# Rows of maxima turned by a transposing DMA, and the last maxima combined right behind the last unit

## The chip, the cores and the metric

The kernel runs on one core of a Trainium2 chip. The metric is the device time of one execution in microseconds; the kernel before took 875.57 us (median of 3 runs, 874.52 to 877.58). Engines: TensorE (PE; PEld its weight loads), VectorE (DVE), ScalarE (ACT), GpSimd (POOL) and SyncE (SP), which here issues every DMA.

## The reference, cut to what matters

```python
x = L0_attn_x                       # (4, 1024, 256) f32
xn = layernorm(x)
q, kv = rotary(heads(xn @ Wq)) * 16 ** -0.5, rotary(heads(xn @ Wkv))    # 16 heads of 16
att = einsum('bmd,bnd->bmn', q, kv)             # 1024 x 1024 for each of 64 (batch, head)
out = softmax(att) @ kv                          # keys are the values too
ffn = (silu(xn @ wg.T) * (xn @ wu.T)) @ wd.T     # hidden 768, dequantised int weights
return x + out @ Wout + bout + ffn
```

## The kernel before

The front part (to about 230 us) runs over 8 chunks of 512 tokens: layernorm, projections, rotary tables and the whole feed-forward. The projected q and k are split into two 16-bit parts each and stored to DRAM. The rest is the attention, and it is this part that the change is about.

**Pairs and steps.** The 64 (batch, head) items go by in 32 pairs (`PAIRS`), two heads at a time on different rows of TensorE. A pair has 8 steps (`STEPS`), one for each tile of 128 keys, and each step two halves of 512 queries. So a pair has 16 half steps. A half step on TensorE (`step`, L777) is: `scores` (L703, matmuls L716), a part of `values` (L734, probabilities times values) and `maxima` (L740, matmuls L751).

**Why maxima.** The softmax subtracts each query's maximum before the exponential. The maxima are made by a first pass over the scores with the queries on the partitions: `maxima` on TensorE, then one VectorE reduce of 128 x 1024 per unit (L1137), 16 units a pair. This pass runs 12 steps (`LEAD`) ahead of the second. So unit 15 of pair p + 1 stands in half step 7 of pair p (counted from 0), and behind it start the units of pair p + 2. VectorE's `combine` (L1142, the operation L1147) folds the two halves of the keys into `rowmax`. In the kernel before, `combine` of a pair stands behind the first reduce of the following pair.

**How the maxima reach the scores.** GpSimd's `split_max` (L1291) writes `rowmax` as three 16-bit parts into 48 columns of `mparts` (six small operations, L1299 to L1309). The parts must become rows of `qs`, where they are multiplied by unit rows in `ks`, so that the score matmul of 51 rows gives score minus maximum. The turn is done by `turn_max` (L649) on TensorE with an identity, in step 6 (`T_AT`) of the pair before, behind the values of half step 12. It goes into a score bank. ScalarE's `rows` (L915, operation L922) copies 48 rows out to `mrows`, and SyncE's `load_mrows` (L372, two DMAs at L377) puts them into `qs` and raises `m_in`. `scores` waits for `m_in` once a pair, before its first half step.

**Banks.** Scores rotate over three PSUM banks, 4 to 6 (`score_bank`, L344). `place` (L333) numbers everything that takes one: two places for each half step, one for the turn (`turn_place`, L338) and, from pair 10 (`LAG`) on, one for an output tile (`tile_place`, L341). `free` (L686) makes TensorE wait until the use three places ago is read: an exponential, a copy of the turned rows or a copy of a tile. The banks 0 to 3 are for maxima, bank 7 for the values.

**ScalarE** does 32 exponentials a pair (L972), a copy of the pair's outputs (L986) in step 1, and from pair 10 on the copy of a tile (L992). **VectorE** does also one small reciprocal a pair (`invert`, L1192, operation L1197) in step 4.

**SyncE** works through one fixed list (`slot`, L465), in this order for pair p: loads of an output tile's parts (`load_tile`, L400, from pair 10 on); `load_pair` of pair p + 2; `store_o` of pair p - 1; `store_inv` of pair p - 1 (waits for the reciprocal); `store_res` of a tile; `load_mrows` of pair p + 1. GpSimd multiplies the tile's parts (L1339); TensorE projects the tile in half step 3 (L759).

Of the kernel before, what the change touches and what calls it, by code (L numbers as in the profile page):

```python
# [23 lines left out]
FP16 = mybir.dt.float16  # L24
# [30 lines left out]
M_UNIT = (2.0 ** 15, 2.0 ** 5, 1.0)  # L55
MAXES = 2 * BT
LEAD = 12
T_AT = 6
INV_AT = 4
COPY_O_AT = 1  # L60
TILE_SLOT = 3
# [7 lines left out]
QH = SEQ // CHUNK  # L69
PER_STEP = 2 * QH  # L70
PBUF = 4
TURN_INDEX = PER_STEP * T_AT + 2
TILE_INDEX = 2 * (TILE_SLOT + 1)
WHOLE = None
VALUES = {PBUF + n: divmod(n, 2) for n in range(2 * STEPS)}
# [11 lines left out]
def build(nc, x, w_q, w_kv, w_out, b_out, w_gate, w_up, w_down, rope, ident, out):  # L87
# [10 lines left out]
    with ExitStack() as ctx:  # L98
# [78 lines left out]
        munit = sb("munit", [P, 4, 2, BT], F32)  # L177
        mrest = sb("mrest", [P, 2, BT], F32)
        mparts = [sb(f"mparts{i}", [P, P], FP16) for i in range(2)]
        mrows = [sb(f"mrows{i}", [MPARTS * MAXES, P], FP16) for i in range(2)]  # L180
        used[0] = 0
        probs = [carve(CHUNK, F32) for _ in range(PBUF * PER_STEP)]
        vstage = [carve(2 * BT * 2 * DH, F32, "p (a k n) -> p a k n", a=2, k=BT) for _ in range(2)]
# [74 lines left out]
        msplit = sem("msplit")  # L258
        msplit_done = sem("msplit_done")
        mturned = sem("mturned")  # L260
        mrows_done = sem("mrows_done")
        m_in = [sem(f"m_in{i}") for i in range(RING)]
        scores_done = sem("scores_done")
        exp_done = sem("exp_done")
# [63 lines left out]

        def pair_base(p):

            return (PER_STEP * STEPS + 1) * p + max(p - LAG, 0)

        def place(p, kt, j):  # L333

            n = PER_STEP * kt + j
            return pair_base(p) + n + (n >= TILE_INDEX) * with_tile(p) + (n >= TURN_INDEX) * (p + 1 < PAIRS)

        def turn_place(p):  # L338
            return pair_base(p) + TURN_INDEX + with_tile(p)

        def tile_place(p):  # L341
            return pair_base(p) + TILE_INDEX
# [5 lines left out]
        def _(sp):  # L348
# [10 lines left out]
            def load_pair(p, ring):  # L359
# [4 lines left out]
                for a in range(2):  # L364
# [3 lines left out]
                    for tile, first, part in ((qs, 0, q[0:DH, :]), (qs, DH, q), (ks, 0, k), (ks, 2 * DH, k[0:DH, :])):  # L368
                        n = part.shape[0]
                        sp.dma_start(tile[ring][top + first:top + first + n, :], part).then_inc(stacks_in[ring], 16)  # L370

            def load_mrows(p, slot):  # L372
                sp.wait_ge(mrows_done, p + 1)
                n = MPARTS * BT
                for a in range(2):
                    top = HEAD_ROWS * a + PROD
                    sp.dma_start(qs[slot % RING][top:top + MPARTS, :], mrows[slot % 2][a * n:(a + 1) * n, :]  # L377
                                 ).then_inc(m_in[slot % RING], 16)

            def store_o(p, slot):  # L380
# [68 lines left out]
                load_pair(p, p)  # L449
            for c in range(CPB, NCHUNK):  # L450
                if c + 1 == NCHUNK:
                    load_mrows(0, 0)
                store_chunk(c // CPB, c % CPB)

# [10 lines left out]
            def slot(p, j, load, rows, tiles):  # L465

                for b, t, n, k in tiles:
                    sp.wait_ge(divided, CREDIT + n - 1)
                    if n is tiles[0][2]:

                        m = (j + 1) % 2
                        sp.wait_ge(inv_stored[m], 16 * QH * ((p - 3 - m) // 2 + 1))
                    load_tile(b, t, k)
                if p == PAIRS - 2:
                    sp.wait_ge(inv_stored[0], 16 * QH * (PAIRS - RING) // 2)
                    load_last(0, front_in)
                if load:
                    if not isinstance(p, int) or p >= 2:
                        sp.wait_ge(scores_done, QH * STEPS * (p - 1))
                    load_pair(p + 2, (j + 2) % RING)  # L480
                if not isinstance(p, int) or p >= 1:
                    store_o(p - 1, j - 1)
                if not isinstance(p, int) or p >= 1:
                    store_inv(p - 1, j - 1)
                for b, t, n, k in tiles:
                    store_res(b, t, n, k)
                if rows:
                    load_mrows(p + 1, j + 1)
# [40 lines left out]
        def _(pe):  # L529
# [60 lines left out]
            def turn_qk(c):  # L590

                pe.wait_ge(rope_done, CT * (c + 1))
                if c < NCHUNK - 1:
                    pe.wait_ge(xl_ready, KD * (c + 2))
                else:
                    pe.wait_ge(mrows_done, 1)
                for g in range(4):
                    if g == 2:
                        pe.wait_ge(silu_done, KH * c + 5)
                        pe.wait_ge(hid_done, KH * c + 5)  # L600
                    for t in range(CT):
                        mm = pe.transpose(bank_turn(g)[:, t * P:(t + 1) * P], qk[:, t, g * P:(g + 1) * P], identf[:, :])  # L602
                    mm.then_inc(turned, 1)
# [42 lines left out]
                                   ks[pl][top:top + PROD, h * CHUNK:(h + 1) * CHUNK], start=True, stop=True)  # L646
                mm.then_inc(max_scores, 1)

            def turn_max(p, slot_of, before, bank):  # L649

                pe.wait_ge(msplit_done, p + 1)
                pe.wait_ge(*before)
                pe.transpose(ps[:, bank, 0:P // 2].bitcast(FP16), mparts[slot_of % 2][:, :], identh[:, :]
                             ).then_inc(mturned, 1)

            pe.wait_ge(ident_in, 16)
            turn_x(0)
            pe.wait_ge(wqkv_in, 32)
# [3 lines left out]
            for c in range(NCHUNK):  # L662
                project(c)
                if c == 0:
                    pe.wait_ge(wsum_done, 2)
                else:
                    for t in range(CT):
                        down(c - 1, t)
                gate_up(c, 0)
                gate_up(c, 1)  # L670
                if c + 1 < NCHUNK:
                    turn_x(c + 1)
                else:
                    pe.wait_ge(identh_ready, 1)
                    turn_max(0, 0, (y_done, CT * c), 4)
                units = lead_units(c)
                for j in range(2, KH):
                    if units:
                        if j == 2:
                            pe.wait_ge(rope_read, CT * (c + 1))  # L680
                        lead(units[j - 2])
                    gate_up(c, j)
                turn_qk(c)


            def free(p, first, last):  # L686

                exps = 0
                for n in range(max(first, 0), last + 1):
                    q = p - (n < pair_base(p))  # L690
                    if q + 1 < PAIRS and n == turn_place(q):
                        pe.wait_ge(mrows_done, q + 2)
                    elif with_tile(q) and n == tile_place(q):
                        pe.wait_ge(wout_copied, q - LAG + 1)
                    else:
                        k = n - pair_base(q)
                        k -= with_tile(q) and k > TILE_INDEX
                        k -= q + 1 < PAIRS and k > TURN_INDEX
                        exps = PER_STEP * STEPS * q + k + 1
                if exps:  # L700
                    pe.wait_ge(exp_done, exps)
# [75 lines left out]
            def step(turn, ls, last_turn=False):  # L777
# [5 lines left out]
                for half in range(2):  # L783
# [6 lines left out]
                        values(of, pair, *block)  # L790
                    elif p == 0 and slot:
                        if slot == 1:
                            pe.wait_ge(y_done, CT * NCHUNK)
                        for k in range(KD):
                            pe.matmul(ps[:, 7, :], identh[:, :], wg[:, k, 0:CHUNK], start=True, stop=True)
                    if p + 1 == PAIRS:
# [6 lines left out]
                            project_tile(n, n % 2, 0)  # L803
                        if slot in FRONT_AT:
                            project_front(FRONT_AT[slot])
                    if slot == 2 * T_AT and p + 1 < PAIRS:
                        turn_max(p + 1, pl + 1, (exp_done, PER_STEP * (STEPS * p + T_AT)), score_bank(turn_place(p)))
                    if slot == TILE_SLOT and with_tile(p):
                        free(p, tile_place(p) - 3, tile_place(p) - 3)
                        project_tile(p - LAG, (p - LAG) % 2, score_bank(tile_place(p)))  # L810
# [51 lines left out]
        def _(act):  # L862
# [52 lines left out]
            def rows(p, slot, turn, bank):  # L915

                act.wait_ge(mturned, p + 1)
                if not (isinstance(p, int) and p < 2):

                    act.wait_ge(m_in[(slot - 2) % RING], 32 * (turn + (slot - 2) // RING + 1))  # L920
                n = MPARTS * MAXES
                act.activation(mrows[slot % 2][:, :], ps[0:n, bank, 0:P // 2].bitcast(FP16), ACT.Copy  # L922
                               ).then_inc(mrows_done, 1)

            roots(0, CT)
            normalise(0)
            roots(CT, 2 * CT)
# [4 lines left out]
            for c in range(NCHUNK):  # L932
# [7 lines left out]
                high(c, 0)  # L940
                if more:
                    copy_x(c + 1, 0)
                else:
                    rows(0, 0, 0, 4)
                high(c, 1)
                silu(c, 2)
                if more:
# [13 lines left out]
            def exps(turn, ls):  # L961
# [5 lines left out]
                for j in range(PER_STEP):  # L967
# [10 lines left out]
                    if j == 1 and kt == T_AT and p + 1 < PAIRS:  # L978
                        rows(p + 1, pl + 1, turn, score_bank(turn_place(p)))

            def copy_o(p, slot, turn):

# [22 lines left out]
        def _(dve):  # L1005
# [125 lines left out]
            def maxima(turn, m, h, bank):  # L1131
# [4 lines left out]
                dve.wait_ge(max_scores, n + 1)  # L1136
                dve.tensor_reduce(negmax[pl % 2][:, h, :, kt], ps[:, bank:bank + 2, :],  # L1137
                                  AX.X, ALU.max, negate=True).then_inc(max_done, 1)
                if k == 0 and not (isinstance(p, int) and p == 0):
                    combine(p - 1, pl - 1)  # L1140

            def combine(p, pl):  # L1142

# [59 lines left out]
            def step(turn, ls, last_turn=False):  # L1203
                m = ls + LEAD
                q = ls // STEPS
                if not last_turn or m < RING * STEPS:
                    maxima(turn, m, 0, 0)
                    maxima(turn, m, 1, 2)
                if last_turn and m == RING * STEPS:
                    combine(PAIRS - 1, RING - 1)  # L1210
# [42 lines left out]
        def _(pool):  # L1253
# [37 lines left out]
            def split_max(p, slot):  # L1291

                pool.wait_ge(rowmax_done, p + 1)
                if not (isinstance(p, int) and p < 2):
                    pool.wait_ge(mturned, p - 1)
                rm = rowmax[slot % 2][:, :, :]
                mp = mparts[slot % 2][:, 0:2 * MPARTS * BT].rearrange("p (a k i) -> p a k i", a=2, k=MPARTS)
                n = 5 * p
# [119 lines left out]
```

## Time and profile before

| | |
|---|---|
| time, median of 3 | 875.57 us |
| profiled execution | 875.66 us |
| its span | 873.9 us |
| granted TensorE clock, mean | 0.996 |
| busy: PE, DVE, ACT, POOL | 836.4, 762.1, 692.8, 187.2 us |
| chain that ended last: PE, ACT, DVE | 66%, 24%, 4% of the span |
| VectorE reduces L1137 | 512, 1217 ns mean, 596.2 us |
| ScalarE exponentials L972 | 1024, 595 ns mean, 557.8 us |
| TensorE values L734, scores L716, maxima L751 | 326.5, 198.2, 190.2 us |
| SyncE waited for the copy of the turned rows, before L377 | 46.3 us in 32 times |
| SyncE waited for the reciprocal, before L397 | 182.8 us in 30 times |

An operation's busy time is that of the engine; its mean may be longer than the time from one start to the next, since an instruction begins before the one ahead of it has ended. The loop's half steps are regular, so the distance of equal rows (start to start) tells the cost better than the durations.

### The profile page before, as it was taken

To read this page: it belongs to the slowest core of one execution; us is meant where nothing else is said; L and a number is where in the kernel's file an instruction comes from. 1 tells how busy PE (TensorE), PEld (TensorE's weight loads), DVE (VectorE), ACT (ScalarE), POOL (GpSimd) and SP (SyncE) were. 2 spreads that over 40 slices of the span, in tenths; PEclk is the share of its full clock that TensorE was granted. 3 is DMA by queue.
4 is the path that set the end of the run, shared out by engine and by line. 5 is a ranking of instruction groups with operands and counts; after the bars stand their busy time and mean duration, and the time that the engine had idled before them with its cause. 6 is when DMAs were issued, how large, how long until landed. Compare 5 with 4: busy or idle time off the path is not lost.

```text
span 873.9 us, 19473 instructions
## 1 busy us (share of the span) xinstructions
PE 836.4 (96%) x7488; PEld 326.0 (37%) x7488; DVE 762.1 (87%) x936; ACT 692.8 (79%) x1303; POOL 187.2 (21%) x411
## 2 busy tenths in 40 slices
PE   4898999999999999999999999999999999999998
PEld 2465555555433333333333333333333333333334
DVE  6897888788799999999999999999999999999902
ACT  4545445433799999999999999999999999999983
POOL 4523344435210000001111111111111111111210
PEclk9899999999999999999999999999999999999999
DMA  9112110011201111111112211111111221111222
GB/s 316 47 50 78 57 50 27 23 49 49 67 26 28 35 37 27 32 28 27 45 49 55 57 50 50 46 46 45 45 51 51 53 57 49 50 46 46 75 75 79
DMA packets 58498, 47.46 MB, mean 54 GB/s; under 512 B 18189, under 2 KB 48717, under 8 KB 58405
## 3 DMA queue, kind: packets, MB, share of 16 engines
q1 hardware_dynamic: 58404, 46.20, 18.1%
q8 instruction: 60, 0.98, 0.5%
q14 instruction: 34, 0.27, 0.1%
HBM read 28.57 MB, written 16.90 MB: 52 GB/s over the span
## 4 chain that ended last, share of the span: by engine, by line
PE 66%; ACT 24%; DVE 4%; issue 4%; POOL 0%; ACTq 0%; DVEq 0%
ACT arena L972 23%; PE ps L734 20%; PE ps L751 11%; PE ps L716 11%; PE ps L585 7%; PE ps L613 4%; PE ps L759 3%; PE ps L562 2%; PE ps L564 1%; PE ps L563 1%; PE ps L602 1%; PE ps L645 1%; DVE stats L1013 1%; DVE negmax L1137 1%; DVE side L1071 1%
## 5 line engine op out<-in xcount | busy, mean ns | idle before, releaser
L1137 DVE TENSOR_REDUCE negmax<-ps 128x2 f32<-128x1024 f32 x512 | 596.2, 1217 | 31.8 <-PE ps L751 27.7
L972 ACT ACTIVATE arena<-ps 128x512 f32<-128x512 f32 x1024 | 557.8, 595 | 49.4 <-PE ps L716 25.8
L734 PE MATMUL ps<-arena 128*32 128x256 f32 x4072 | 326.5, 392 | 2.2 <-issue 2.0
L716 PE MATMUL ps<-qs,ks 51*128 51x512 f16 x1024 | 198.2, 382 | 9.6 <-ACT arena L972 8.6
L751 PE MATMUL ps<-ks,qs 48*128 48x512 f16 x976 | 190.2, 386 | 0.0
L734 PEld LDWEIGHTS ps<-arena 128*32 128x32 f32 x4072 | 80.3, 107 | 122.6 <-issue 121.5
L751 PEld LDWEIGHTS ps<-ks,qs 48*128 48x128 f16 x976 | 46.7, 92 | 188.5 <-issue 183.2
L899 ACT ACTIVATE side<-ps 128x512 f32<-128x512 f32 x48 | 28.7, 597 | 94.8 <-PE ps L585 94.8
L585 PE MATMUL ps<-arena,side 128*128 128x512 f16 x384 | 89.0, 380 | 0.2
L716 PEld LDWEIGHTS ps<-qs,ks 51*128 51x128 f16 x1024 | 51.6, 93 | 91.5 <-ACT arena L972 53.8
L1299 POOL TENSOR_TENSOR mparts<-rowmax,munit 128x16 f16<-128x16 f32 x32 | 7.6, 238 | 291.8 <-DVE rowmax L1147 291.8
L1277 POOL TENSOR_TENSOR side<-side 128x512 f16<-128x512 f32 x48 | 55.9, 1167 | 61.1 <-ACT side L905 60.3
L585 PEld LDWEIGHTS ps<-arena,side 128*128 128x128 f16 x384 | 35.4, 98 | 44.4 <-issue 6.3
L1339 POOL TENSOR_TENSOR arena<-arena 128x256 f32<-128x256 f32 x24 | 17.5, 730 | 158.2 <-DMA arena<-inv_d 158.2
L1071 DVE SCALAR_TENSOR_TENSOR side<-ps,side 128x512 f32<-128x512 f32 x48 | 32.9, 690 | 16.0 <-PE ps L585 9.5
L905 ACT ACTIVATE side<-side 128x512 f16<-128x512 f32 x48 | 30.0, 625 | 13.5 <-DVE side L1071 13.3
L613 PE MATMUL ps<-side 128*128 128x256 f16 x336 | 37.8, 273 | 0.0
L613 PEld LDWEIGHTS ps<-side 128*128 128x128 f16 x336 | 32.9, 98 | 5.3
L1344 POOL TENSOR_TENSOR arena<-arena,x_all 128x256 f32<-128x256 f32 x22 | 16.1, 731 | 64.6 <-ACT arena L992 64.6
L759 PE MATMUL ps<-wo,arena 128*128 128x256 f32 x96 | 27.1, 405 | 0.0
L562 PE MATMUL ps<-arena 128*128 128x512 f16 x56 | 22.2, 397 | 4.5 <-DVE side L1071 4.5
L1077 DVE TENSOR_TENSOR arena<-ps,arena 128x512 f16<-128x512 f32 x32 | 19.8, 682 | 7.1 <-ACT arena L913 7.1
(101 smaller groups left out, 522.7 us busy)
## 6 DMA issues: line engine op xcount, KB each, us to landing
parts_d<-arena SPq DMA_DIRECT2D x64, 128.0 KB
x_all<-x_dram SPq DMA_DIRECT2D x8, 512.0 KB, 8.8
qs<-parts_d SPq DMA_DIRECT2D x64, 64.0 KB, 1.9
ks<-parts_d SPq DMA_DIRECT2D x64, 64.0 KB, 1.9
o_d<-arena SPq DMA_DIRECT2D x124, 32.0 KB
arena<-o_d SPq DMA_DIRECT2D x24, 128.0 KB
arena<-inv_d SPq DMA_DIRECT2D x48, 64.0 KB
out_dram<-arena SPq DMA_DIRECT2D x24, 128.0 KB, 1.8
```

The lines of the kernel that those rows point to most:

```text
L562: pe.matmul(bank_proj(t), hi, wqkv_hi[:, k, :], start=(k == 0), stop=False)
L585: mm = pe.matmul(bank, w[:, k, j * P:(j + 1) * P], xp[:, k, :], start=(n == 0), stop=(n == 2 * KD - 1))
L613: mm = pe.matmul(bank_down(c, t), hp[:, n % KH, t * P:(t + 1) * P], wd[:, n % KH, :], start=(n == 0), stop=(n == 2 * KH - 1))
L716: mm = pe.matmul(ps[:, score_bank(place(p, kt, 2 * half + a)), :], ks[ring][top:top + ROWS, kt * P:(kt + 1) * P], qs[ring][top:top + ROWS, ...
L734: mm = pe.matmul(ps[32 * j:32 * j + 32, 7, cols], vstage[pl % 2][:, j % 2, kt, :], probs[PER_STEP * (kt % PBUF) + j][:, cols], start=(kt = ...
L751: mm = pe.matmul(ps[:, 2 * h + a, :], qs[ring][top:top + PROD, kt * P:(kt + 1) * P], ks[ring][top:top + PROD, h * CHUNK:(h + 1) * CHUNK], ...
L759: mm = pe.matmul(ps[:, bank, 0:DIM], atile[k][:, g, :], wo[:, g, :], start=(g == 0), stop=(g == HG - 1))
L905: act.activation(hh[:, j, :], hid[j % 3][:, :], ACT.Copy).then_inc(hh_done, 1)
L972: act.activation(probs[PER_STEP * (kt % PBUF) + j], ps[:, score_bank(place(p, kt, j)), :], ACT.Exp).then_inc(exp_done, 1)
L1071: dve.scalar_tensor_tensor(hid[j % 3][:, :], bank_up(j), DEQUANT * H_SCALE, gact[j % 2][:, :], ALU.mult, ALU.mult).then_inc(hid_done, 1)
L1137: dve.tensor_reduce(negmax[pl % 2][:, h, :, kt], ps[:, bank:bank + 2, :], AX.X, ALU.max, negate=True).then_inc(max_done, 1)
L1277: pool.tensor_tensor(hl[:, j, :], hid[j % 3][:, :], hh[:, j, :], ALU.subtract).then_inc(hl_done, 1)
```

## The change

The turn on TensorE and ScalarE's copy go, and with them their place in the rotation of banks. In their stead SyncE issues one transposing DMA of the whole 128 x 128 16-bit tile `mparts` into `mrows` (`turn_rows`), from SBUF to SBUF. It waits for `split_max` and, from pair 2 on, for the load that read this `mrows` before. It stands in SyncE's list behind `store_o` and ahead of `store_inv`. `load_mrows` now waits for the DMA's landing (`mturned`, 16 a time). GpSimd's guard before it writes `mparts` again waits for the same semaphore. VectorE's `combine` now stands right behind unit 15 of its own pair; it waits for that very reduce. In the front part the last chunk loses a turn and a copy, and `turn_rows(0, 0)` goes ahead of `load_mrows(0, 0)`.

```diff
-T_AT = 6
-TURN_INDEX = PER_STEP * T_AT + 2
@@
-        mrows = [sb(f"mrows{i}", [MPARTS * MAXES, P], FP16) for i in range(2)]
+        mrows = [sb(f"mrows{i}", [P, 1, P], FP16) for i in range(2)]
@@
         def pair_base(p):
-            return (PER_STEP * STEPS + 1) * p + max(p - LAG, 0)
+            return PER_STEP * STEPS * p + max(p - LAG, 0)
         def place(p, kt, j):
             n = PER_STEP * kt + j
-            return pair_base(p) + n + (n >= TILE_INDEX) * with_tile(p) + (n >= TURN_INDEX) * (p + 1 < PAIRS)
+            return pair_base(p) + n + (n >= TILE_INDEX) * with_tile(p)
@@ SyncE
+            def turn_rows(p, slot):
+                sp.wait_ge(msplit_done, p + 1)
+                if p >= 2:
+                    sp.wait_ge(m_in[(slot - 2) % RING], 32 * ((p - 2) // RING + 1))
+                sp.dma_start_transpose(mrows[slot % 2][:, :, :], mparts[slot % 2][:, :]).then_inc(mturned, 16)
             def load_mrows(p, slot):
-                sp.wait_ge(mrows_done, p + 1)
+                sp.wait_ge(mturned, 16 * (p + 1))
@@
                 if not isinstance(p, int) or p >= 1:
                     store_o(p - 1, j - 1)
+                if rows:
+                    turn_rows(p + 1, j + 1)
                 if not isinstance(p, int) or p >= 1:
                     store_inv(p - 1, j - 1)
@@ TensorE: turn_max and its two calls go; turn_qk of the last chunk
-                    pe.wait_ge(mrows_done, 1)
+                    pe.wait_ge(y_done, CT * c)
@@ TensorE, free
-                    if q + 1 < PAIRS and n == turn_place(q):
-                        pe.wait_ge(mrows_done, q + 2)
@@ ScalarE: rows and its two calls go
@@ VectorE, maxima
-                if k == 0 and not (isinstance(p, int) and p == 0):
-                    combine(p - 1, pl - 1)
+                if k + 1 == MAXES:
+                    combine(p, pl)
@@ GpSimd, split_max
-                    pool.wait_ge(mturned, p - 1)
+                    pool.wait_ge(mturned, 16 * (p - 1))
```

## Rows read from the trace of the kernel before

**Rows 1.** The page, busy us (share of the span) and instructions of each engine

```profile
PE 836.4 (96%) x7488; PEld 326.0 (37%) x7488; DVE 762.1 (87%) x936; ACT 692.8 (79%) x1303; POOL 187.2 (21%) x411
```

**Rows 2.** Windows: stretch, length, busy us by engine, granted clock, DMA share, GB/s

```profile
300.00:400.00 100.00, 97.75 (x1014) 30.26 (x1014) 98.02 (x95) 94.22 (x180) 9.56 (x43) 1.00 0.12 30
500.00:600.00 100.00, 98.78 (x997) 32.47 (x995) 94.10 (x91) 92.95 (x178) 16.29 (x50) 1.00 0.19 50
```

**Rows 3.** Timeline of ScalarE: start, us, engine, line, operation, tiles, count

```profile
320.64 0.26 ACT L922 ACTIVATE mrows<-ps 48x128 f16<-48x128 f16 x1
339.68 0.26 ACT L922 ACTIVATE mrows<-ps 48x128 f16<-48x128 f16 x1
...
494.97 0.26 ACT L922 ACTIVATE mrows<-ps 48x128 f16<-48x128 f16 x1
...
514.75 0.26 ACT L922 ACTIVATE mrows<-ps 48x128 f16<-48x128 f16 x1
```

**Rows 4.** Timeline of TensorE around the turn of a tile pair

```profile
507.68 0.39 PE L716 MATMUL ps<-qs,ks 51*128 51x512 f16 x2
...
513.30 0.38 PE L716 MATMUL ps<-qs,ks 51*128 51x512 f16 x2
...
514.18 0.23 PE L653 MATMUL ps<-identh,mparts 128*128 128x128 f16 x1
...
514.92 0.39 PE L716 MATMUL ps<-qs,ks 51*128 51x512 f16 x2 [0.19 <-ACT arena L972]
...
518.41 0.39 PE L716 MATMUL ps<-qs,ks 51*128 51x512 f16 x2
```

**Rows 5.** Timeline of VectorE, in the same pair and at the start

```profile
507.89 2.35 DVE L1137 TENSOR_REDUCE negmax<-ps 128x2 f32<-128x1024 f32 x2
...
511.28 0.17 DVE L1147 TENSOR_TENSOR rowmax<-negmax 128x16 f32<-128x16 f32 x1
511.36 1.22 DVE L1137 TENSOR_REDUCE negmax<-ps 128x2 f32<-128x1024 f32 x1
512.50 0.24 DVE L1197 RECIPROCAL arena<-arena 128x16 f32<-128x16 f32 x1
512.65 3.42 DVE L1137 TENSOR_REDUCE negmax<-ps 128x2 f32<-128x1024 f32 x3
...
7.03 0.18 DVE L1022 RECIPROCAL rstd<-std 128x4 f32<-128x4 f32 x1 [0.36 <-ACT std L865]
7.24 0.16 DVE L1024 SCALAR_TENSOR_TENSOR shift<-mv,rstd 128x4 f32<-128x4 f32 x1
```

**Rows 6.** Timeline of TensorE in a pair without a tile

```profile
328.81 0.38 PE L716 MATMUL ps<-qs,ks 51*128 51x512 f16 x2
...
330.35 0.39 PE L716 MATMUL ps<-qs,ks 51*128 51x512 f16 x2
```

**Rows 7.** Timeline of GpSimd

```profile
511.52 0.22 POOL L1299 TENSOR_TENSOR mparts<-rowmax,munit 128x16 f16<-128x16 f32 x1 [6.26 <-DVE rowmax L1147]
...
513.02 0.22 POOL L1309 TENSOR_TENSOR mparts<-mrest,mwhole 128x16 f16<-128x16 f32 x1
...
520.96 0.73 POOL L1339 TENSOR_TENSOR arena<-arena 128x256 f32<-128x256 f32 x1 [7.25 <-DMA arena<-inv_d]
```

**Rows 8.** Timeline of SyncE's queue: the time is that of issuing

```profile
512.76 1.15 SPq L397 DMA_DIRECT2D inv_d<-arena  x2
513.96 0.43 SPq L415 DMA_DIRECT2D out_dram<-arena  x1
515.04 1.54 SPq L377 DMA_DIRECT2D qs<-mrows  x2
...
517.12 1.33 SPq L407 DMA_DIRECT2D arena<-inv_d  x2
```

**Rows 9.** DMA issues by line, whole execution: count, KB each, median us to landing

```profile
qs<-parts_d SPq DMA_DIRECT2D x64, 32.0 KB, 1.8
```

**Rows 10.** Timeline, weight loads of the next tile's projection

```profile
522.69 0.73 PEld L759 LDWEIGHTS ps<-wo,arena 128*128 128x128 f32 x4 [0.41 <-ACT arena L972]
```

More of the change, by code:

```diff
@@ L260, in build @@
         mturned = sem("mturned")
-        mrows_done = sem("mrows_done")
         m_in = [sem(f"m_in{i}") for i in range(RING)]
@@ L329, in pair_base @@
         def pair_base(p):
-            return (PER_STEP * STEPS + 1) * p + max(p - LAG, 0)
+            return PER_STEP * STEPS * p + max(p - LAG, 0)
         def place(p, kt, j):
             n = PER_STEP * kt + j
-            return pair_base(p) + n + (n >= TILE_INDEX) * with_tile(p) + (n >= TURN_INDEX) * (p + 1 < PAIRS)
-        def turn_place(p):
-            return pair_base(p) + TURN_INDEX + with_tile(p)
+            return pair_base(p) + n + (n >= TILE_INDEX) * with_tile(p)
         def tile_place(p):
@@ L376, in load_mrows @@
                     top = HEAD_ROWS * a + PROD
-                    sp.dma_start(qs[slot % RING][top:top + MPARTS, :], mrows[slot % 2][a * n:(a + 1) * n, :]
+                    sp.dma_start(qs[slot % RING][top:top + MPARTS, :], mrows[slot % 2][a * n:(a + 1) * n, 0, :]
                                  ).then_inc(m_in[slot % RING], 16)
@@ L451, in _ @@
                 if c + 1 == NCHUNK:
+                    turn_rows(0, 0)
                     load_mrows(0, 0)
@@ L647, in lead @@
                 mm.then_inc(max_scores, 1)
[L649 to L654, printed above, removed]
             pe.wait_ge(ident_in, 16)
@@ L672, in _ @@
                     turn_x(c + 1)
-                else:
-                    pe.wait_ge(identh_ready, 1)
-                    turn_max(0, 0, (y_done, CT * c), 4)
                 units = lead_units(c)
@@ L690, in free @@
                     q = p - (n < pair_base(p))
-                    if q + 1 < PAIRS and n == turn_place(q):
-                        pe.wait_ge(mrows_done, q + 2)
-                    elif with_tile(q) and n == tile_place(q):
+                    if with_tile(q) and n == tile_place(q):
                         pe.wait_ge(wout_copied, q - LAG + 1)
@@ L697, in free @@
                         k -= with_tile(q) and k > TILE_INDEX
-                        k -= q + 1 < PAIRS and k > TURN_INDEX
                         exps = PER_STEP * STEPS * q + k + 1
@@ L792, in step @@
                         if slot == 1:
+                            pe.wait_ge(identh_ready, 1)
                             pe.wait_ge(y_done, CT * NCHUNK)
@@ L805, in step @@
                             project_front(FRONT_AT[slot])
-                    if slot == 2 * T_AT and p + 1 < PAIRS:
-                        turn_max(p + 1, pl + 1, (exp_done, PER_STEP * (STEPS * p + T_AT)), score_bank(turn_place(p)))
                     if slot == TILE_SLOT and with_tile(p):
@@ L913, in high_qk @@
                     act.activation(parts[g][:, 0, :], bank_turn(g), ACT.Copy).then_inc(hi_done, 1)
[L915 to L923, printed above, removed]
             roots(0, CT)
@@ L942, in _ @@
                     copy_x(c + 1, 0)
-                else:
-                    rows(0, 0, 0, 4)
                 high(c, 1)
@@ L977, in exps @@
                         copy_tile(p - LAG, (p - LAG) % 2, score_bank(tile_place(p)))
-                    if j == 1 and kt == T_AT and p + 1 < PAIRS:
-                        rows(p + 1, pl + 1, turn, score_bank(turn_place(p)))
             def copy_o(p, slot, turn):
@@ L1208, in step @@
                     maxima(turn, m, 1, 2)
-                if last_turn and m == RING * STEPS:
-                    combine(PAIRS - 1, RING - 1)
                 if ls % STEPS == INV_AT and (q or not isinstance(turn, int)) and not (last_turn and q == RING - 1):
```

## The prediction

> **What bounds the kernel now.** I read the page first. PE is busy in nearly the whole span, DVE and ACT follow [rows 1]. That share doesn't name the bound, so I read windows next. In 300 to 400 us (head pairs 0 to 9, which have no output tile) PE is busy 97.75 and DVE 98.02 of 100 us: two engines near the limit. In 500 to 600 us (with tiles) PE has 98.78, DVE only 94.10 [rows 2]. The granted clock is 1.00, the 2.4 GHz level, in both, so the clock is no term of the sum.
>
> Then the period. ScalarE's copy of the turned maxima comes once a pair: every 339.68 - 320.64 = 19.04 us without a tile and every 514.75 - 494.97 = 19.78 us with one [rows 3]. A pair is 16 half steps: scores, values, maxima. TensorE's timeline shows what a half step costs and what the turn adds. From 507.68 to 513.30 five half steps take 5.62 us, 1.124 each. The four that follow, the turn in the first, take 518.41 - 513.30 = 5.11 us in place of 4.50: 0.61 us extra, though the transpose itself is 0.23 us long [rows 4]. The rest is a wait: the turn takes one of the three score banks, so the scores at 514.92 stood for ScalarE ("<-ACT arena L972"). They needed an exponential that is one later than usual.
>
> **The change, part by part.**
>
> 1. *The turn and its copy go (31 times in the loop, pairs 0 to 30; each serves the next pair).* The gain on TensorE lies between 0.50 us (the turn's own half step, 514.92 - 513.30 = 1.62 against 1.12) and 0.61 us (all four) [rows 4]. Slower half steps stand only behind the turn, so I take 0.57. ScalarE also loses its 0.26 us copy [rows 3]; it is not the bound, so this counts nothing beyond the bank that comes free sooner.
>
> 2. *What is late next, tile pairs.* VectorE: back to back, two reduces take 2.35 us and one takes 1.22, so each costs 1.13; the combine costs 511.36 - 511.28 = 0.08 and the reciprocal 512.65 - 512.50 = 0.15 [rows 5]. That is 16 x 1.13 + 0.23 = 18.31 us a pair, under 19.78 - 0.57 = 19.21. TensorE stays the bound and the 0.57 is kept: 21 pairs x 0.57 = 12.0 us.
>
> 3. *Pairs without a tile.* TensorE needs 16 x 1.124 plus what the copy of the outputs makes it wait once (330.35 - 328.81 = 1.54 against 1.12, 0.42) [rows 6]: 18.40 us. VectorE needs 18.31 plus the new wait of item 4, 18.43. The two are level, and each holds up the other now and then; I take 18.52, a gain of 0.52 of 19.04. Ten pairs: 5.2 us.
>
> 4. *The combine right behind the last unit.* It now waits for the reduce issued just ahead of it; before, the next pair's first reduce stood between. Queued behind the wait is that reduce, and TensorE's maxima two units on wait for it. The nearest row of such a self-wait is the reciprocal at 7.03, 0.18 long, with its reader at 7.24: 0.03 us after its end, where neighbours without a wait overlap by 0.09 (512.74 against 512.65) [rows 5]. So 0.12 us a pair on VectorE, bounds 0 and 0.15; hidden in tile pairs by the slack of item 2, counted in item 3. In return the row maxima are there one reduce earlier.
>
> 5. *The transposing DMA, which no row shows.* I follow the chain in the tile pair at 510 us. The last reduce of the next pair ends at 507.89 + 2.35 = 510.24 [rows 5]. Combine, 0.03 + 0.17: 510.44. GpSimd's split starts 0.07 later (511.52 after 511.28 + 0.17) and takes 513.02 + 0.22 - 511.52 = 1.72 [rows 7]: 512.23. SyncE issues at 512.27. The load of the turned rows has two issues, 1.54 us together [rows 8]; the second starts 0.77 in and lands as a small load does, 1.8 to 1.9 us on [rows 9]: 2.7 us. The next pair's scores, at 518.41 before, are wanted at 518.41 - 0.60 = 517.81; less 2.7 and 0.1 for the semaphore, the load must start by 515.0. So the transposition may take 2.7 us from issue to landing. Everything beyond stalls TensorE one for one in all 31 pairs, as it waits in order and nothing can take the slot. Lower bound of its latency: 1.8 us, the load of a similar size [rows 9]. Upper bound: the slowest landing inside the loop, the broadcast load, issued from 517.12 and used at 520.96 by GpSimd, 3.8 us [rows 7, 8]. The size is 32 KB, nearest to the 32 KB load, and it has no HBM side; the reordering costs something. I take 2.4 us: no stall.
>
> What I set beside this: the DMA load of 32 KB lands in 1.8 us [rows 9]. The Trainium skill ("VectorE: DVE Perf Modes", The three transpose paths) gives 1309 ns for a 128 x 128 16-bit transpose by DMA and 390 ns on TensorE, and advises TensorE where PSUM will do, so it speaks against the change; "DMA: Bandwidth & Descriptors", Anatomy of one DMA, gives about 2.0 us of fixed cost, for another issuing path than SyncE's; no run here shows either figure yet. Added, an estimate from these pages is 3.3 us, a stall of 0.6 us a pair, and the sum would come to about 877.
>
> 6. *SyncE's queue.* The transposition stands ahead of store_inv, store_res and load_mrows. It is issued at 512.27, before the 512.76 at which store_inv began [rows 8], and takes between 0.43 us (the issue of store_res, at 513.96) and 0.77 (half of the load's 1.54). So store_inv moves to 513.0 at the latest, store_res ends by 514.7, and the load still finds the queue free by 515.0. The next tile's loads follow the load of the rows as before; its product is ready at 520.96 + 0.73 = 521.69, and TensorE wants it at 522.69 [rows 7, 10]. Of the 1.0 us of slack the shorter pair takes 0.6. Nothing for the queue, then; its cover is gone if the issue takes over 1.1 us, after which it is a stall like item 5's. GpSimd's new wait (the transposition of two pairs before) is two periods, some 38 us, old: free.
>
> 7. *The first part.* One transposition and one copy go from the last chunk: at most 0.23 + 0.26 us, I take 0.3. The new load is issued earlier there, long before pair 0 starts.
>
> **The sum.** The profiled execution took 875.66 us (span 873.9 and 1.8 around it), 0.1 over the median of 875.57. 875.66 - 12.0 - 5.2 - 0.3 = 858.2 us.
>
> **The rivals.**
>
> *A transposition somewhat slow.* At 3.0 us the stall is 0.3 us in 31 pairs: 9.3 us back, 867.5. It gives between all and almost none of the gain back as the latency goes from 2.7 to 3.3. For it: the move rearranges 16-bit elements; against it: plain small transfers land at 1.8 to 1.9, so 0.8 us more is needed before anything shows. The Trainium skill's figures, added as above, fall at its upper end.
>
> *A transposition so slow that the kernel loses.* The gain of 17.5 us is used up by a stall of 0.56 us, a latency of 3.3; from 3.4 on the kernel is measurably slower than before. At the 3.8 us of the slowest landing it stalls 1.1 us x 31 = 34 us: 892. Its place is the first scores of each pair, the wait for m_in. For it: the budget of 2.7 is a chain without any slack, which was 0.6 us with the copy through PSUM; the transposition and the load are two landings in series where one was. Against: it needs twice a small load's latency.
>
> *VectorE becomes the bound everywhere.* If the self-wait costs far more than 0.15 us, the pairs without tile gain only half, 2.6 us less: 861. It stays inside the forecast's range.
>
> *The change does little* because the 0.61 us is not the turn's: then half steps 13 to 16 stay at 1.15 and the gain is 0.50 a pair, 31 x 0.50 + 0.3 = 15.8: 859.9; also within it.
>
> **How the numbers follow.** No stall (the last two included): 0.50, with 856.5 to 863 as its own range (0.60 in all 31 pairs gives 875.66 - 18.6 - 0.5 = 856.6). Somewhat slow: 0.25. Slow enough to lose: 0.25. About 0.3%, 2.6 us, is what a measurement of this kernel can tell from no change. Faster by more holds all of the first and 0.20 of the second: 0.70. Within 0.3%: 0.05 of the second and 0.01 of the third, 0.06. Slower: 0.24. The range runs from 856.5 to 886; its upper end is a stall of 0.9 us (858.2 + 27.9), a latency of 3.6, and beyond it I leave 0.17, with 0.02 below.
>
> **What would show it.** In the profile after, the copies of the output banks should lie 18.5 us apart early and 19.2 us later, all 16 half steps at 1.12, no wait of the scores for "DMA qs<-mrows", the split about 1.0 us earlier in the pair, and VectorE near 98% in both parts. A wait of L716 for that DMA, once a pair, is the stall; its length plus 2.7 is the transposition's latency. If SyncE's row for the new issue is longer than 1.1 us, item 6 is wrong. If the gap at 514 us is gone but the slots behind stay at 1.15, item 1's upper part is.

## The result

The changed kernel takes 870.16 us (median of 7 runs, 867.68 to 872.65), the kernel before took 877.58 us in the same comparison (7 runs). The ratio is 0.993 with a 95% interval of 0.9914 to 0.9946: faster by 0.7%, 5 to 8 us; the two medians lie 7.4 us apart. Forecast were 858.2 us and a gain of 17.5. So the sign and the range held, and more than half of the gain is missing. The question is where it went.

The page of the changed kernel's profile (its execution took 867.68 us), busy time by engine and the chain that ended last:

```profile
span 865.9 us, 19347 instructions
...
PE 826.8 (95%) x7456; PEld 320.8 (37%) x7456; DVE 758.0 (88%) x936; ACT 688.0 (79%) x1271; POOL 185.9 (21%) x411
...
PE 71%; DVE 15%; DMA 3%; SPq 2%; issue 2%; ACT 2%; POOL 2%; DVEq 0%; ACTq 0%; POOLq 0%
```

Against [rows 1], PE is busy 9.6 us less. New in the chain is DMA with SyncE's queue, 5% of the span: something that TensorE waits for is now a transfer. ScalarE's 24% of before is down to 2%. TensorE's score matmuls wait for an exponential 9 times where they did 40 times before, 31 fewer: the wait behind the turn, once a pair, is gone. Windows of the same two stretches as in [rows 2]:

```profile
300.00:400.00 100.00, 97.67 (x1028) 29.94 (x1028) 98.51 (x98) 94.79 (x177) 9.12 (x41) 1.00 0.14 32
500.00:600.00 100.00, 98.97 (x998) 32.46 (x998) 94.36 (x92) 93.39 (x176) 16.88 (x51) 1.00 0.20 52
```

More matmuls fit into the head pairs' 100 us (1028 against 1014), yet both engines show idle time. The list of waits names it (engine, line, waited for: us in total, times, longest):

```profile
PEld ps L743 <- DVE negmax L1114: 109.9, 270, 0.4
...
PEld ps L708 <- DMA qs<-mrows: 14.3, 26, 1.7
...
PE ps L708 <- DMA qs<-mrows: 6.0, 8, 1.3
```

L708 is the score matmul (L716 before), and it waits for the load of the turned rows in nearly every pair. In the kernel before the same wait stood there once, with 0.7 us. The 109.9 us of weight loads that wait for VectorE look worse but cost nothing that shows: they are 0.4 us at most, and the half steps below are no longer for them.

TensorE's timeline at the end of a tile pair, to set beside [rows 4]:

```profile
512.54 0.38 PE L708 MATMUL ps<-qs,ks 51*128 51x512 f16 x2
...
513.68 0.39 PE L708 MATMUL ps<-qs,ks 51*128 51x512 f16 x2
...
514.96 0.39 PE L708 MATMUL ps<-qs,ks 51*128 51x512 f16 x2
...
516.10 0.39 PE L708 MATMUL ps<-qs,ks 51*128 51x512 f16 x2
```

The half steps take 1.14, 1.28, 1.14 us. The one with the turn, 1.62 before, is now 1.14, and the one behind it went from 1.17 to 1.12. The last one before the next pair took 1.17 before the change and takes 1.17 where nothing disturbs it, not the 1.12 that was forecast for all sixteen; here it takes 1.28, and in other pairs up to 2.58. The half steps with other work are as they were: 1.54 with the copy of the outputs, 2.18 and 1.22 with an output tile. Over the 31 pair changes of this execution the surpluses of the last half steps over 1.17 us add up to 9.0 us. Since 867.7 - 9.0 = 858.7, the sum of the forecast is there, and the stalls are what is missing: between the two profiled executions the gain is 8.0 of the 17.5 us, and 9.0 of the 9.5 that are missing are these surpluses. The table sorts them by what the trace shows at the place:

| where | pairs | stall |
|---|---|---|
| pairs 1, 3, 5, 7, 18, 27: the transposition lands 3.3 to 4.0 us after its issue | 6 | 5.1 us |
| pairs 9, 11, 29: its issue takes 1.43 to 1.73 us, in place of 1.14 | 3 | 1.0 us |
| pairs 12 to 17, 20 to 26, 28, 30 (tile pairs): nothing unusual, 0.10 to 0.16 each | 15 | 1.9 us |
| pair 31: GpSimd's split takes 2.5 us | 1 | 1.0 us |
| pairs 2, 4, 6, 8, 10, 19 | 6 | 0 |

For the transposing DMA itself the view of the tile `mrows` gives the issue on SyncE (ns, min/median/max) and the time to landing:

```profile
L371 SPq DMA_TRANSPOSE mrows<-mparts x32: 1119/1143/1728, 204.8 to 822.1; - x32
...
DMA to landing us min/median/max: 2.3/2.3/4.0
```

A median of 2.3 us where I had taken 2.4, but a tail to 4.0; and an issue of 1.14 us where I had taken at most 0.77. What that does to SyncE's queue in a tile pair:

```profile
509.32 1.14 SPq L371 DMA_TRANSPOSE mrows<-mparts  x1
510.51 1.14 SPq L399 DMA_DIRECT2D inv_d<-arena  x2
511.70 0.43 SPq L417 DMA_DIRECT2D out_dram<-arena  x1
512.18 1.55 SPq L379 DMA_DIRECT2D qs<-mrows  x2
```

The rows have landed at 509.32 + 2.3 = 511.6, but SyncE gets to their load only at 512.18, 2.86 us after the issue. The rows are in place 2.73 us later, at 514.91, and the scores start at 514.96. Without a tile there is no L417 row, and the load starts at 2.34.

The combine came out as worked out. VectorE and GpSimd in the same pair:

```profile
503.74 3.49 DVE L1114 TENSOR_REDUCE negmax<-ps 128x2 f32<-128x1024 f32 x3
507.33 0.17 DVE L1124 TENSOR_TENSOR rowmax<-negmax 128x16 f32<-128x16 f32 x1
507.42 2.35 DVE L1114 TENSOR_REDUCE negmax<-ps 128x2 f32<-128x1024 f32 x2
...
509.07 0.22 POOL L1284 TENSOR_TENSOR mparts<-mrest,mwhole 128x16 f16<-128x16 f32 x1
```

The last reduce ends at 507.23; combine and wait take until 507.42. A reduce right behind a reduce would have started 0.09 us before 507.23, so the two cost 0.28 us; the combine alone cost 0.08 before [rows 5]. The self-wait is thus 0.20 us, not 0.12. The split ends at 509.29, 2.06 us after the last reduce (1.99 were forecast), and the issue follows at 509.32.

### The profile page after: what moved, and what is told of

It reads as the page before. It is cut to its first block, busy times and chain, and to the rows that moved or that the text cites. A ratio compares the mean times of both kernels' runs of the same rounds, so it can differ in the third digit from the quotient of the medians.

```text
span 865.9 us, 19347 instructions
## 1 busy us (share of the span) xinstructions
PE 826.8 (95%) x7456; PEld 320.8 (37%) x7456; DVE 758.0 (88%) x936; ACT 688.0 (79%) x1271; POOL 185.9 (21%) x411
## 4 chain that ended last, share of the span: by engine, by line
PE 71%; DVE 15%; DMA 3%; SPq 2%; issue 2%; ACT 2%; POOL 2%; DVEq 0%; ACTq 0%; POOLq 0%
PE ps L726 24%; PE ps L743 13%; DVE negmax L1114 12%; PE ps L708 11%; PE ps L590 8%; PE ps L618 4%; PE ps L751 3%; DMA qs<-mrows 2%; DMA mrows<-mparts 2%; ACT arena L951 2%; PE ps L567 1%; PE ps L568 1%; PE ps L569 1%; PE ps L607 1%; PE ps L650 1%
## 5 line engine op out<-in xcount | busy, mean ns | idle before, releaser
L1114 DVE TENSOR_REDUCE negmax<-ps 128x2 f32<-128x1024 f32 x512 | 589.9, 1212 | 23.8 <-PE ps L743 19.6
L708 PE MATMUL ps<-qs,ks 51*128 51x512 f16 x1024 | 197.8, 382 | 9.6 <-DMA qs<-mrows 6.0
L743 PEld LDWEIGHTS ps<-ks,qs 48*128 48x128 f16 x976 | 46.6, 92 | 198.9 <-DVE negmax L1114 109.9
L708 PEld LDWEIGHTS ps<-qs,ks 51*128 51x128 f16 x1024 | 49.8, 92 | 89.5 <-ACT arena L951 45.1
L567 PE MATMUL ps<-arena 128*128 128x512 f16 x56 | 21.8, 389 | 4.5 <-DVE side L1048 4.5
```

Source lines behind the costliest of these rows:

```text
L567: pe.matmul(bank_proj(t), hi, wqkv_hi[:, k, :], start=(k == 0), stop=False)
L708: mm = pe.matmul(ps[:, score_bank(place(p, kt, 2 * half + a)), :], ks[ring][top:top + ROWS, kt * P:(kt + 1) * P], qs[ring][top:top + ROWS, ...
L743: mm = pe.matmul(ps[:, 2 * h + a, :], qs[ring][top:top + PROD, kt * P:(kt + 1) * P], ks[ring][top:top + PROD, h * CHUNK:(h + 1) * CHUNK], ...
```

## The experiments

**Where the wait comes from: the queue, the chain, or VectorE.** The first moves one entry of SyncE's list.

```diff
@@ slot (SyncE), label e2_load_before_res
-                for b, t, n, k in tiles:
-                    store_res(b, t, n, k)
                 if rows:
                     load_mrows(p + 1, j + 1)
+                for b, t, n, k in tiles:
+                    store_res(b, t, n, k)
```

> The changed kernel with one thing moved: SyncE loads the turned rows ahead of the store of the output tile, not behind it. Theory A (the wait for the rows is what gives the gain back, and in pairs with a tile it is SyncE's queue: the transposition's issue takes 1.14 us, store_inv 1.14 and store_res 0.43, so the load starts 2.86 us after the transposition's issue though that lands after 2.28): the last half step of the 21 tile pairs falls from 1.28 to 1.33 us to 1.17, the load starts 2.34 us after the transposition's issue, and the kernel is 3 to 4 us faster than the changed one, 11 us under the kernel before. The landings of 3.3 to 4.0 us in a few pairs stay, shorter in effect by 0.4. Theory B (the landing of the transposition itself is the bound in every pair): no change, since the queue isn't waited for. Theory C (VectorE, which now waits for its own reduce): no change.

Measured: 866.76 us (6 runs) against 876.48 for the kernel before (17 runs), ratio 0.9885 [0.986, 0.9911]. SyncE's queue in a tile pair, and the waits of the whole kernel:

```profile
490.95 1.14 SPq L371 DMA_TRANSPOSE mrows<-mparts  x1
492.14 1.14 SPq L399 DMA_DIRECT2D inv_d<-arena  x2
493.33 1.55 SPq L379 DMA_DIRECT2D qs<-mrows  x2
494.93 0.42 SPq L417 DMA_DIRECT2D out_dram<-arena  x1
```

```profile
PEld ps L708 <- DMA qs<-mrows: 6.8, 9, 1.6
...
PE ps L708 <- DMA qs<-mrows: 3.9, 5, 1.3
```

The load starts 2.38 us after the issue, and the last half step of an undisturbed tile pair is 1.17. The waits fall from 26 times to 9. Seven last half steps are still long: six behind a late landing and the one before pair 31. The gain over the kernel before is 9.7 us where 11 were expected. Theory A holds for the tile pairs; B and C had expected no change. As ratios to the kernel before, 0.9885 here and 0.993 for the changed kernel, the move is worth 4 us, the upper end of what was expected; the two intervals almost touch, so the trace is the better witness.

**The chain has no slack.** The DMA stays and the combine goes back behind the next pair's first reduce.

```diff
@@ maxima (VectorE), label e3_late_combine
-                if k + 1 == MAXES:
-                    combine(p, pl)
+                if k == 0 and not (isinstance(p, int) and p == 0):
+                    combine(p - 1, pl - 1)
@@ step (VectorE)
+                if last_turn and m == RING * STEPS:
+                    combine(PAIRS - 1, RING - 1)
```

> The changed kernel with the combine back in its old place, behind the next pair's first reduce. Theory A (the chain from the last reduce to the scores has no slack left): the chain starts 0.97 us later and the stall before each pair grows by that, less the 0.5 us of slack in the even pairs without a tile: 31 x 0.97 - 2.5 = 27 us more than the changed kernel, some 20 us over the kernel before. Theory C (the new wait of VectorE is what costs): the kernel gets faster than the changed one by about 0.12 x 31 = 4 us.

Measured: 892.61 us (4 runs), ratio 1.0178 [1.0143, 1.0213]: 16 us slower than the kernel before and 22 slower than the changed one (27 were expected). A pair's first scores and the waits:

```profile
504.71 0.39 PE L708 MATMUL ps<-qs,ks 51*128 51x512 f16 x2 [0.97 <-DMA qs<-mrows]
```

```profile
PEld ps L708 <- DMA qs<-mrows: 37.1, 31, 2.0
...
PE ps L708 <- DMA qs<-mrows: 27.8, 31, 1.7
```

All 31 pairs wait. The last half step is 2.21 to 2.29 us in most tile pairs, 1.05 over the undisturbed 1.17; the stalls add up to 30.8 us, 21.8 more than in the changed kernel. In an undisturbed tile pair that is the one-for-one price of a chain that starts about a microsecond later. The sum stays 5 us under the expectation mostly because pairs 3, 5, 7, 18 and 27 have no late landing of 3 us or more in this run, and because nothing moved in pair 31, which has no pair behind it to wait for. Theory C is out: VectorE's self-wait is gone here, and the kernel is slower.

**The combine alone.** The same move in the kernel before, with the turn on TensorE.

```diff
@@ maxima (VectorE), label e4_combine_only, from the kernel before
-                if k == 0 and not (isinstance(p, int) and p == 0):
-                    combine(p - 1, pl - 1)
+                if k + 1 == MAXES:
+                    combine(p, pl)
@@ step (VectorE)
-                if last_turn and m == RING * STEPS:
-                    combine(PAIRS - 1, RING - 1)
```

> The kernel before with only the combine moved right behind the last reduce of its pair; the turn stays on TensorE. Theory A: nothing, within 1 us of the kernel before, as the turn stands at a fixed place in TensorE's order and the rows had about 0.6 us of slack. Theory C (the self-wait of VectorE costs in each pair): 2 to 4 us slower. The period stays 19.04 and 19.79 us.

Measured: 876.48 us (12 runs), ratio 0.9989 [0.9972, 1.0006]. No change, with periods of 19.04 and 19.79 us. The self-wait does not show, and an earlier combine is worth nothing to a turn that stands at a fixed place of TensorE's order. It is worth 22 us to the DMA. The second half of the change is what makes the first one pay.

**The turn's removal with slack.** The maxima run 13 steps ahead; two more units are done in front, where TensorE and VectorE wait for each other.

```diff
@@ label e6_lead13
-LEAD = 12
+LEAD = 13
@@ TensorE, ahead of down_most of the last chunk
+            pe.wait_ge(silu_done, KH * NCHUNK)
+            pe.wait_ge(hid_done, KH * NCHUNK)
+            maxima(0, LEAD - 1, 0)
+            maxima(0, LEAD - 1, 1)
@@ VectorE, between low_qk and add_ffn of the last chunk
+            maxima(0, LEAD - 1, 0, 0)
+            maxima(0, LEAD - 1, 1, 2)
```

> The changed kernel with the maxima 13 steps ahead in place of 12: the two units more are done before the first step, between the last storing of parts and the last feed-forward sums. So the chain to the rows starts one step, 2.25 us, earlier in each pair. Theory A: no stall before any pair is left, also not where the transposition lands after 3.3 to 4.0 us; the periods are 18.5 and 19.2 us, and the gain of taking the turn from TensorE stands whole: 31 stalls of together 9.0 us go, less 0 to 2.3 us for the two units in front; 16 to 18 us under the kernel before. Theory C: as the changed kernel, 7 us under the kernel before. If TensorE's removed half-step time were only 0.50 us a pair and not 0.60, 13 to 14 us under.

Measured: 859.13 us (5 runs, 857.28 to 861.17), ratio 0.9806 [0.9782, 0.983], 17.3 us under the kernel before. One window of this kernel, the waits of its score matmuls, and SyncE's queue in a tile pair:

```profile
500.00:600.00 100.00, 99.86 (x1022) 32.72 (x1018) 96.19 (x95) 94.86 (x178) 18.08 (x58) 1.00 0.19 51
```

```profile
PEld ps L708 <- ACT arena L955: 46.1, 237, 0.7
...
PEld ps L708 <- issue: 12.2, 58, 0.7
PE ps L708 <- ACT arena L955: 2.1, 9, 0.6
PEld ps L708 <- DVE x_all L1066: 1.0, 1, 1.0
```

```profile
444.94 1.15 SPq L371 DMA_TRANSPOSE mrows<-mparts  x1
447.83 1.15 SPq L399 DMA_DIRECT2D inv_d<-arena  x2
449.02 0.43 SPq L417 DMA_DIRECT2D out_dram<-arena  x1
449.51 1.56 SPq L379 DMA_DIRECT2D qs<-mrows  x2
```

No wait for `mrows` is left, though three transpositions here land after 3.3 to 3.6 us. The reason is in the queue: store_inv waits for its reciprocal until 447.83, 2.89 us after the issue, so a late landing hides behind it. The load lands at 449.51 + 2.73 = 452.24, half a microsecond ahead of the scores at 452.73. The periods are 18.49 and 19.24 us, 0.55 less than before in both kinds of pair, and PE is busy 99.86 of 100. No cost of the two units in front can be seen: pair 0 starts at 229.66 us in this execution and at 229.67 in the kernel before, though between traces with one and the same front part this start moves by up to 2.5 us. This version beats both kernels.

**Is it the earlier maxima that help?** The same 13 steps and early combine with the turn on TensorE and ScalarE.

```diff
@@ label e7_lead13_te: e4_combine_only, and the edit of e6_lead13 (cut to its first lines)
-LEAD = 12
+LEAD = 13
```

> The kernel before (turn on TensorE and ScalarE) with the combine right behind its last reduce and the maxima 13 steps ahead, as in the version with 13 steps and the DMA. If the gain of that version is the turn's removal, this one stays within 2 us of the kernel before, with periods of 19.04 and 19.79 us. If it is the earlier maxima that helped, it is 10 us or more under the kernel before.

Measured: 876.27 us (10 runs) against 876.26, ratio 1.0007 [0.9991, 1.0023]. With the turn on TensorE the 13 steps and the early combine are worth nothing. The 17 us are the turn's removal, once its chain has slack.

**Why some transpositions are late.** The changed kernel again, for a second trace and a comparison on one chip:

> The changed kernel as it is, on the chip of this call. Its time over the kernel before is to be 6 to 8 us less, as before. Theory F (late landings of the transposition come from fetches of instructions): each transposition with a landing above 3.2 us has a 16 KB packet of the instruction queue on a DMA engine that began 0.7 to 1.7 us after the issue, and none of the others has.

Measured: 870.35 us (6 runs), ratio 0.993 [0.9907, 0.9953]. Its stalls add up to 10.1 us. The expectation held only in part. Late landings and fetches of 16 KB go together, but the stated window of 0.7 to 1.7 us was too narrow: pair 1 is late with a fetch at 1.81, pair 25 with one at 2.43, and pair 27, with one at 0.89, lands after 3.01, under the 3.2 that was set. The DMA view of two stretches of the first trace of the changed kernel, each 3.5 us from the issue in pair 3 and pair 4 (queue, kind, packets, MB, share of 16 engines; then the median us to landing):

```profile
q8 instruction: 1, 0.02, 2.2%
...
mrows<-mparts SPq DMA_TRANSPOSE x1, 3.3
```

```profile
q14 instruction: 1, 0.01, 1.0%
...
mrows<-mparts SPq DMA_TRANSPOSE x1, 2.3
```

In pair 3 a fetch of 16 KB of instructions runs as one packet: 2.2% of 16 engines x 3.5 us is 1.2 us on a single DMA engine. By the packet records it began 0.87 us after the transposition's issue and ended at 2.11. The 8 KB fetch in pair 4 did no harm. The packets of the transposition itself show what the fetch does. It moves as 128 packets of 256 bytes and 32 of 4 bytes. The same view of 0.4 us, from 1.1 us after the issue, first in pair 3 and then in pair 4:

```profile
DMA packets 120, 0.03 MB, mean 77 GB/s; under 512 B 120, under 2 KB 120, under 8 KB 120
```

```profile
DMA packets 128, 0.03 MB, mean 82 GB/s; under 512 B 128, under 2 KB 128, under 8 KB 128
```

In pair 3, 8 of the 128 are missing, the share of one DMA engine in 16. They move from 2.10 us on, when the fetch has ended.

The test shifts the fetches: small matmuls ahead of the last feed-forward sums move TensorE's position in its instructions against the work.

```diff
@@ TensorE, ahead of down_most of the last chunk, label e8_pad_te (e9_pad24: 24 in place of 48)
+            pe.wait_ge(identh_ready, 1)
+            pe.wait_ge(silu_done, KH * NCHUNK)
+            pe.wait_ge(hid_done, KH * NCHUNK)
+            for _ in range(48):
+                pe.matmul(ps[:, 1, 0:2], identh[:, :], identh[:, 0:2], start=True, stop=True)
```

> The changed kernel with 48 matmuls of two columns (96 instructions) more on TensorE ahead of the last feed-forward sums, where TensorE mostly waits. They shift the later fetches of TensorE's instructions against the work: by 96 instructions, some 4.6 us earlier. Theory F: the fetch that met the transposition in pairs 3, 5 and 7 comes 3 to 4 us before its issue, these three land after 2.3 us and the last half step ahead of them falls from 1.68 to 1.91 us to 1.17; which later pairs are met changes too. Rival G (the odd pairs are late because of the loads of the pair ahead or the parity of a buffer): pairs 3, 5 and 7 stay late at 3.3 to 3.8 us. Total: 2 us faster to 4 us slower than the changed kernel.

> As the one with 48, with 24 small matmuls (48 instructions), a shift of some 2.3 us. Theory F: the fetches of pairs 3, 5 and 7 begin 0.6 to 1.5 us ahead of the issue; the landing is 2.3 us, or the issue itself takes up to 0.6 us longer where the fetch still runs. Rival G: late as before.

Measured: 870.88 us (10 runs), ratio 0.9946 [0.9924, 0.9968], with 48; 864.95 us (2 runs), ratio 0.987 [0.985, 0.9891], with 24. Landing of the transposition, us from issue, in the pairs that the test was about:

```
pair                3      5      7
changed           3.33   3.26   3.78
changed, again    3.46   3.52   3.67
24 matmuls more   2.29   2.28   2.29
48 matmuls more   2.29   2.27   2.34
```

The odd pairs are cured in both, so it is not their parity (rival G). The fetches went where they were expected: in pairs 3, 5 and 7 they begin 3.5 to 3.6 us ahead of the issue with 48 matmuls, and 0.8 to 1.4 us ahead with 24. With 48, other pairs are met: 8, 10, 21, 28 and 30 land after 2.9 to 4.5 us, and nothing is gained in sum. With 24 only 14 and 23 are met, the stalls fall to 5.0 us, and the kernel is 5 us faster than the changed one, in the two executions that there are, for a reason that has nothing to do with its work. All seven traces with the DMA give 217 transpositions behind pair 0. I sorted them by when a 16 KB fetch began, counted from the issue; the bounds of the rows were drawn after looking at the data:

```
fetch began                     transpositions   landed after
0.6 to 2.1 us behind the issue        31         2.89 to 3.99 us, all late
2.1 to 2.5 us behind                  13         2.27 to 2.30, two at 4.4 and 4.5
0.45 us ahead to 0.1 us behind        23         10 by 2.34, 13 from 2.37 to 2.88
none of these                        150         2.27 to 2.34, one at 2.69
```

The packets tell the rows apart better than these bounds do. In 24 of the 33 late ones, with fetches that began at 0.62 to 1.52 us, exactly 8 data packets moved only when the fetch had ended. In the other 9, from 1.56 us on and with the two at 4.4 and 4.5 among them, all data had moved, but 2 of the 32 small packets had not. In the 11 that are not late nothing was held. In all 33 the landing follows 1.0 to 1.3 us behind the end of the fetch (once 1.5). Undisturbed, the last small packet moves at 1.93 us and the landing follows 0.35 later; why it takes longer behind a fetch is not shown, and neither is the cause of the one at 2.69, which held nothing.

With a start ahead of the transposition it is the issue that takes longer, up to 1.73 us. The Trainium skill ("DMA: Bandwidth & Descriptors", Queues, rings and completion order) says that an engine drains a whole packet of one ring before it turns to another; the trace agrees in pair 3, where the 8 packets moved only behind the fetch's one packet of 1.24 us. The load of the rows is spared: all 31 in the kernel before landed 2.68 to 2.76 us after the first issue, also where a fetch began at 0.84, and over eight traces the 27 with a fetch that began 0.6 to 2.1 us behind the first issue landed after 2.69 to 2.81. Each of its two DMAs gives 4 updates of the semaphore at the landing where the transposition gives 16, so it may run on fewer engines; that was not tried.

## Why the prediction was right or wrong, point by point

- **Item 1, the turn's cost** (0.57 us a pair): right in size. 0.55 measured, in the version without stalls. Of the slow half steps behind the turn one fell from 1.17 to 1.12; the last one stays at 1.17, so not all of the 0.61 was the turn's.
- **Items 2 and 3, what is late next**: right. The periods are 18.49 where 18.52 was forecast, and 19.24 where 19.21, in e6_lead13 and, where nothing stalls, in the changed kernel without a tile. VectorE, busy 98.5% in the head pairs, holds up nothing that shows: but for the half steps with the copy or a tile, those of head pairs are as long as those of tile pairs, where VectorE has slack. That the two engines hold each other up, as item 3 said, did not come.
- **Item 4, the self-wait**: mis-sized, 0.20 us against 0.12 and outside its bound of 0.15. Without effect: alone it changes nothing (e4), and the period without a tile is as forecast.
- **Item 5, the transposition's latency**: the budget of 2.7 us was right to a tenth: a load that starts 2.86 us behind the issue holds up the scores by 0.11. The median, 2.28 us, was a little under my 2.4. The step that failed is "I take 2.4 us: no stall": it took one value for something with a tail. My bounds, 1.8 and 3.8 us, nearly held the whole spread of 2.3 to 4.0, but I read them as two possible constants; with a budget 0.4 us above the median, one late landing in five pairs gives back 5.1 us. The profile of before held a sign of the cause: its page lists 60 packets of the instruction queue with 0.98 MB, 16 KB each.
- **Item 6, SyncE's queue**: failed. The issue was put at 0.43 to 0.77 us by the rows of plain DMAs and takes 1.14. "Nothing for the queue" is the second step that failed. The text named over 1.1 us as the point where the cover is gone, and it is: 1.9 us in 15 tile pairs, 1.0 more where a fetch makes the issue longer still.
- **Item 7, the front part** (0.3 us gained): not seen. Pair 0 starts at 229.92 us, against 229.67 before; in four traces with the front part of the changed kernel it starts at 229.92 to 232.37, so 0.3 us can't be told.
- **Pair 31** was not in the text: its chain has a slower split, 2.5 us in place of 1.7, as GpSimd's first two operations take 0.72 and 0.54 us. They take as long in the trace of the kernel before, where the forecast could have read them. The cause wasn't tried. It costs 1.0 us once.
- **The rivals.** "Somewhat slow" gave 867.5 us for 0.3 us of stall in each pair; measured are 0.29 on average (9.0 in 31), and 870. The time is that rival's by luck, its mechanism only in part: not a slow move but a late one now and then, and a queue. "VectorE becomes the bound everywhere" did not come: the self-wait is over 0.15 us, at 0.20, but not by far. The 1.3 us for the move (the Trainium skill, "VectorE: DVE Perf Modes", The three transpose paths) and the 2.0 of fixed cost, stated for another issuing path (the Trainium skill, "DMA: Bandwidth & Descriptors", Anatomy of one DMA), added, gave an estimate of 3.3; measured are 2.3, so they don't add here. The advice to turn on TensorE where PSUM will do (the Trainium skill, "VectorE: DVE Perf Modes", Rules for kernel authors) is borne out in this kernel only where the DMA's chain starts too late (e3_late_combine, 16 us slower than the turn on TensorE). With slack the DMA gains 17, because the turn had cost a wait for a bank and not only 0.23 us of matmul.

## What to carry to other kernels

Work that goes from a busy engine to a DMA gets a latency with a tail: compare the budget of its chain with the worst landing, not with the median, and if it is short start the chain a step earlier, which showed no cost here and was worth 11 us. Price the issue of a new kind of DMA as unknown, and look at what stands between it and the load that reads its result in the same queue. An operation that takes a place in a rotation of banks costs the wait that it makes too, here 0.55 us in all for 0.23 us of matmul; and a part of a change that does nothing by itself (the early combine) can be what the other part lives on.

## What the runs showed of the hardware

- The transposing DMA of 128 x 128 16-bit elements, SBUF to SBUF: 1.12 to 1.14 us to issue on SyncE, 2.28 us from issue to landing when undisturbed. The issues of the plain DMAs beside it in the queue mostly take 0.4 to 0.8 us.
- One 16 KB fetch of instructions takes a DMA engine for 0.9 to 1.5 us where it met a transposition (up to 2.0 elsewhere). A transposition that meets it lands 0.6 to 1.7 us later, and twice 2.1 to 2.2; one engine's share of its packets (8 of 128, or 2 of the 32 small ones) waits for the fetch's end. With 48 more instructions on TensorE (24 matmuls) the kernel was 5 us faster in two executions, more than the change's interval is wide, and its stalls were 4 to 5 us shorter. A difference of half a per cent between two kernels of this kind can come from such a shift.
- A reduce's reader on VectorE that waits for it starts 0.10 us after its end, and the wait costs 0.20 us in all.
